# Another order for the start of a fused attention and ternary-FFN kernel: k first, q and v in one chain, the FFN weights' sums later

## The reference, cut to what matters

```python
# x: (8, 1024, 512) f32;  H = 8 heads of 64, segments of L = 128 tokens
q, k, v = xs @ Wq, xs @ Wk, xs @ Wv
# per segment, carrying a memory (mem, z) along the sequence:
sq, sk = elu(q) + 1, elu(k) + 1
att_mem = sq @ mem / (sq @ z)
mem, z  = mem + sk^T v, z + sum(sk)
att     = gate * att_mem + (1 - gate) * softmax(q k^T / 8) @ v
x = layernorm(x + att @ Wo)

def _quantize(W):                       # a threshold over the whole matrix
    gamma = mean(abs(W))
    return clip(round(W / (gamma + 1e-5)), -1, 1)
h = relu(x @ _quantize(W1)^T + b1)      # W1: (2048, 512)
x = layernorm(x + h @ _quantize(W2)^T + b2)   # W2: (512, 2048)
```

## Time and profile before

| What | Value |
|---|---|
| time, median of 3 runs | 1899.68 us |
| profiled execution, its time | 1899.23 us |
| profiled execution, its span | 1897.3 us |
| PE busy | 1851.0 us, 98% of the span |
| DVE, ACT, POOL busy | 1447.7, 1002.5, 765.9 us |
| granted PE clock, mean | 0.992 of full |

### The profile page before, as it was taken

How to read it: one execution, slowest core, us unless ns; L and a number is a source line. 1 busy time by engine, 2 the same in 40 slices (tenths; PEclk the granted TensorE clock), 3 DMA queues, 4 the chain that set the end, 5 groups by cost and what they waited for, 6 DMA issues and landing times.

```text
span 1897.3 us, 44351 instructions
## 1 busy us (share of the span) xinstructions
PE 1851.0 (98%) x16447; PEld 1307.6 (69%) x16447; DVE 1447.7 (76%) x2935; ACT 1002.5 (53%) x2422; POOL 765.9 (40%) x775
## 2 busy tenths in 40 slices
PE   5789999999999999999999999999999999999998
PEld 3566677766677766677766677766677766677765
DVE  7777777787877787777787877777777777777774
ACT  5755544545555545555545555545555545555541
POOL 1214345444345444335444344444344444344443
PEclk9899999999999999999999999999999999999999
DMA  8412433323333323333323333323333323333110
GB/s 272 124 25 47 63 58 64 65 39 60 63 59 62 62 43 60 63 58 63 67 39 60 64 59 61 68 38 60 60 63 60 69 41 56 60 59 63 35 24 23
DMA packets 556420, 117.47 MB, mean 62 GB/s; under 512 B 529824, under 2 KB 533808, under 8 KB 555696
## 3 DMA queue, kind: packets, MB, share of 16 engines
q1 hardware_dynamic: 556208, 114.64, 31.4%
HBM read 50.54 MB, written 16.80 MB: 35 GB/s over the span
## 4 chain that ended last, share of the span: by engine, by line
PE 93%; DVE 4%; ACT 2%; issue 1%; DMA 0%; POOLq 0%; SPq 0%; DVEq 0%; POOL 0%; ACTq 0%
PE bank L427 12%; PE bank L426 12%; PE bank L440 12%; PE bank L441 11%; PE bank L276 6%; PE bank L278 6%; PE bank L277 6%; PE bank L364 3%; PE bank L409 3%; PE bank L408 3%; PE bank L407 3%; PE bank L290 3%; PE bank L343 3%; PE bank L291 3%; PE bank L292 3%; PE bank L395 2%
## 5 line engine op out<-in xcount | busy, mean ns | idle before, releaser
L426 PE MATMUL bank<-yt,w1t 128*128 128x256 f16 x2048 | 453.9, 273 | 0.2 <-DVE yt L802 0.2
L427 PE MATMUL bank<-yt,w1t 128*128 128x256 f16 x2048 | 453.9, 273 | 0.0
L1145 ACT ACTIVATE prob<-bank,exp_bias,gscalars 128x128 f32<-128x128 f32 x512 | 227.6, 454 | 363.6 <-DVE exp_bias L719 358.6
L440 PE MATMUL bank<-w2t,arena 128*128 128x512 f16 x1024 | 388.4, 379 | 0.0
L441 PE MATMUL bank<-w2t,arena 128*128 128x512 f16 x1024 | 388.1, 379 | 0.0
L1189 ACT ACTIVATE arena<-bank,b_scaled,wscalars 128x256 f32<-128x256 f32 x512 | 263.1, 570 | 207.9 <-PE bank L427 155.0
L854 DVE CAST arena<-arena 128x512 f16<-128x512 f32 x256 | 153.8, 601 | 93.2 <-ACT arena L1189 92.5
L1312 POOL TENSOR_TENSOR att_mem<-att_mem,gate_in 128x512 f32<-128x512 f32 x60 | 87.1, 1452 | 330.9 <-DVE att_mem L758 319.9
L426 PEld LDWEIGHTS bank<-yt,w1t 128*128 128x128 f16 x2048 | 200.4, 98 | 23.5 <-issue 0.6
L427 PEld LDWEIGHTS bank<-yt,w1t 128*128 128x128 f16 x2048 | 200.3, 98 | 22.8
L1390 POOL TENSOR_TENSOR arena<-arena 128x512 f16<-128x512 f32 x128 | 155.2, 1213 | 86.9 <-DVE arena L854 86.9
(11 more groups left out here) (186 smaller groups left out, 4300.4 us busy)
## 6 DMA issues: line engine op xcount, KB each, us to landing
rows<-in_L_attn_x SPq DMA_DIRECT2D x32, 512.0 KB, 3.8
out_rows<-rows SPq DMA_DIRECT2D x64, 256.0 KB, 2.3
x_blocks<-in_L_attn_x SPq DMA_DIRECT2D x248, 64.0 KB, 3.0
sk<-sk_t SPq DMA_DIRECT2D x480, 32.0 KB, 2.0
att_dot<-att_mem SPq DMA_DIRECT2D x480, 32.0 KB, 2.0
y_blocks<-rows SPq DMA_DIRECT2D x480, 32.0 KB
arena<-in_L_ffn_W SPq DMA_DIRECT2D x6, 1024.0 KB, 5.4
w2t<-in_L_ffn_W SPq DMA_DIRECT2D x2, 1024.0 KB, 13.1
```

Of the source, the lines that this page charges most:

```text
L426: pe.matmul(ps[:, c], w1t[:, k, cols], yt[:, g % 2, :, k], start=k == 0, stop=False)
L427: ins = pe.matmul(ps[:, c], w1t[:, k, cols], yt[:, g % 2, :, KT + k], start=False, stop=k == KT - 1)
L440: pe.matmul(banks[own][:], h_hi[:, f, toks], w2t[:, f, :], start=f == 0, stop=False)
L1145: ins = act.activation(prob[:, t, at], ps[:, c], ACT.Exp, scale=gcol(g, G_EXP), bias=exp_bias[:, t, at:at + 1], accum_out=row_sum[:, t, h: ...
```

## The change

Only the order of the first trip changes, with two small joins; POOL and SP keep their lists word for word.

- The chains of q and v become one: PE turns both columns of maxima, the four small operations work on two cells, one product spreads both.
- k's first half is projected on PE ahead of that chain; DVE finds both maxima in a row before it; v's split comes ahead of k's second half; v is projected and split ahead of the first scores.
- o's maximum and chain come behind the first scores' maxima, and o's split on ACT comes behind the whole first softmax.
- ACT's sums, DVE's two sums and `threshold(1)` come later, among and behind the first attention's steps; `ffn_scale` comes behind `round_w(1)`.

```diff
         W_ORDER = "kqvo"
+        CHAINS = ("k", "qv", "o")
+        W_CHAIN = {n: c for c, names in enumerate(CHAINS) for n in names}
...
+            def turn_max(c):
+                if c:
+                    pe.wait_ge(sem["wscale"], c)
+                for i, n in enumerate(CHAINS[c]):
+                    pe.wait_ge(sem["wmax"], W_ORDER.index(n) + 1)
+                    ins = pe.transpose(banks[7][0:1, i * P:(i + 1) * P], w(WMAX[n]), ident32[:])
+                ins.then_inc(sem["wrow"], 1)
...
@@ PE, the loop @@
                 project_qk(g, "k", 0)
                 if g == 0:
-                    turn_max(2)
+                    turn_max(1)
+                    turn_bias()
+                    spread_max(1)
...
+                if g == 0:
+                    project_v(g, 0)
+                    project_v(g, 1)
                 scores(g, 0)
...
+                if g == 0:
+                    turn_max(2)
                 turn_p(g, 0, 0)
                 ffn_down(g - 2, 0, 1)
                 if g == 0:
-                    spread_bias_max()
+                    spread_max(2)
                 ffn_down(g - 2, 0, 2)
                 scores(g, 1)
...
-                if g == 0:
-                    sum_all(1)
                 ffn_down(g - 2, 1, 1)
                 turn_p(g, 0, 1)
+                if g == 0:
+                    sum_all(1)
+                    turn_bias_max()
                 turn_p(g, 1, 0)
+                if g == 0:
+                    spread_bias_max()
                 turn_y(g - 1, 0)
                 turn_p(g, 1, 1)
...
@@ DVE @@
             w_max("q")
-            w_chain("q")
-            w_scale("q")
+            w_max("v")
             for live in range(LIVE):
                 reset_memory(0, live)
-            w_max("v")
-            w_chain("v")
-            w_scale("v")
+            w_chain(1)
+            w_scale(1)
             scalars(0, 0)
             scalars(0, 1)
             scalars(0, 2)
+            w_split("q", 0)
+            w_split("q", 1)
             for g in range(NG + 2):
...
                 qk_split(g, "k", 0)
                 if g == 0:
-                    w_split("q", 1)
+                    w_split("v", 0)
+                    w_split("v", 1)
...
                 if g == 0:
-                    w_scale("o")
+                    v_split(g, 0)
+                    v_split(g, 1)
                 score_max(g, 0, 0)
+                if g == 0:
+                    score_max(g, 0, 1)
+                    w_max("o")
+                    w_chain(2)
                 group_max(g + 1)
                 if g == 0:
+                    w_scale(2)
                     gates()
...
                 score_max(g, 1, 1)
+                if g == 0:
+                    w_sum(2)
+                    w_sum(3)
...
                 p_split(g, 0, 1)
+                if g == 0:
+                    threshold(1)
+                    round_w(0)
+                    round_w(1)
+                    ffn_scale()
...
@@ ACT @@
             w_split("k", 1)
+            w_sum(1, 1)
             w_split("q", 0)
             w_split("q", 1)
             for g in range(NG + 2):
...
                 qk_split(g, "k", 0)
+                if g == 0:
+                    w_split("v", 0)
+                    w_split("v", 1)
                 qk_split(g, "k", 1)
...
                 qk_split(g, "q", 1)
                 if g == 0:
+                    v_split(g, 0)
+                    v_split(g, 1)
                     w_sum(1, 3)
-                    w_sum(1, 0)
-                    w_split("o", 0)
-                    w_sum(1, 2)
                 exponentials(g, 0, 0)
-                v_split(g, 0)
                 if g == 0:
-                    w_split("o", 1)
-                    w_sum(2, 0)
-                exponentials(g, 0, 1)
-                p_split(g, 0, 0)
-                v_split(g, 1)
-                exponentials(g, 1, 0)
-                exponentials(g, 1, 1)
-                p_split(g, 0, 1)
+                exponentials(g, 0, 1)
+                if g == 0:
+                    w_sum(1, 0)
+                p_split(g, 0, 0)
+                exponentials(g, 1, 0)
+                exponentials(g, 1, 1)
+                if g == 0:
+                    w_sum(1, 2)
+                p_split(g, 0, 1)
+                if g == 0:
+                    w_split("o", 0)
+                    w_split("o", 1)
+                    w_sum(2, 0)
+                p_split(g, 1, 0)
+                yt_hi(g - 1, 0)
+                p_split(g, 1, 1)
                 if g == 0:
                     w_sum(2, 1)
                     for n in range(0, 4):
                         put_w(n)
-                p_split(g, 1, 0)
...
```

More of the change, by code:

```diff
@@ L448, in turn_bias, with spread_max @@
                 pe.transpose(banks[6][:, 0:FT], b1_rows[:], ident32[0:FT, 0:FT]).then_inc(sem["bias_turn"], 1)
[L450 to L460, removed]
+            def turn_max(c):
[5 more added lines that the diff above has]
+                ins.then_inc(sem["wrow"], 1)
+            def spread_max(c):
+                first, count = WALL[CHAINS[c][0]], len(CHAINS[c])
+                if c == 0:
                     pe.wait_ge(sem["ones"], 1)
-                pe.wait_ge(sem["wchain"], 4 * at + 4)
-                pe.matmul(banks[7][:, 0:1], ones_all[0:1, :], ws[0:1, WALL[n]:WALL[n] + 1], start=True,
+                pe.wait_ge(sem["wchain"], 4 * c + 4)
+                pe.matmul(banks[7][:, 0:count], ones_all[0:1, :], ws[0:1, first:first + count], start=True,
                           stop=True).then_inc(sem["wall"], 1)
@@ L557, in _ @@
                 ffn_down(g - 2, 1, 0)
+                ffn_down(g - 2, 1, 1)
+                turn_p(g, 0, 1)
                 if g == 0:
                     sum_all(1)
-                ffn_down(g - 2, 1, 1)
-                turn_p(g, 0, 1)
+                    turn_bias_max()
                 turn_p(g, 1, 0)
+                if g == 0:
+                    spread_bias_max()
                 turn_y(g - 1, 0)
@@ L861, in w_max, with w_chain, w_scale @@
                 dve.tensor_reduce(w(WMAX[n]), raw[n], AX_XY, ALU.max, apply_absolute_value=True).then_inc(sem["wmax"], 1)
[L863 to L869, removed]
+            def w_chain(c):
+                first, count = WALL[CHAINS[c][0]], len(CHAINS[c])
+                cell = ws[0:1, first:first + count]
+                dve.wait_ge(sem["wrow"], c + 1)
+                dve.tensor_reduce(cell, banks[7][0:1, 0:count * P].rearrange("p (i n) -> p i n", n=P), AX_X,
+                                  ALU.max).then_inc(sem["wchain"], 1)
+                dve.wait_ge(sem["wchain"], 4 * c + 1)
                 dve.tensor_scalar(cell, cell, 2.0 ** -60, None, ALU.max).then_inc(sem["wchain"], 1)
-                dve.wait_ge(sem["wchain"], 4 * at + 2)
+                dve.wait_ge(sem["wchain"], 4 * c + 2)
                 dve.tensor_scalar(cell.bitcast(U32), cell.bitcast(U32), EXPONENT, None, ALU.bitwise_and).then_inc(sem["wchain"], 1)
-                dve.wait_ge(sem["wchain"], 4 * at + 3)
+                dve.wait_ge(sem["wchain"], 4 * c + 3)
                 dve.tensor_scalar(cell, cell, 2.0 ** -14, None, ALU.mult).then_inc(sem["wchain"], 1)
[L876 to L881, removed]
+            def w_scale(c):
+                inv, scale, count = INV_W[CHAINS[c][0]], SCALE_W[CHAINS[c][0]], len(CHAINS[c])
+                ps = banks[7][:, 0:count]
+                dve.wait_ge(sem["wall"], c + 1)
+                dve.tensor_copy(ws[:, inv:inv + count], ps)
+                dve.reciprocal(ws[:, scale:scale + count], ps).then_inc(sem["wscale"], 1)
             def w_split(n, j):
@@ L1007, in _ @@
                 if g == 0:
+                    w_scale(2)
                     gates()
                 normalise(g - 1, 1, 0)
-                score_max(g, 0, 1)
+                if g:
+                    score_max(g, 0, 1)
                 turn_x(g + 1, 0)
                 turn_x(g + 1, 1)
-                if g == 0:
-                    w_sum(2)
-                    ffn_scale()
                 turn_sk(g)
-                v_split(g, 0)
-                if g == 0:
-                    w_sum(3)
+                if g:
+                    v_split(g, 0)
                 invert_sums(g, 0)
-                if g == 0:
-                    threshold(1)
                 p_split(g, 0, 0)
-                v_split(g, 1)
+                if g:
+                    v_split(g, 1)
                 score_max(g, 1, 0)
```

60 lines of the change are left out of this document (16 added, 44 removed).

## The result

| | before | after |
|---|---|---|
| median (runs) | 1899.68 us | 1912.6 us (1911.59 to 1913.07, 5 runs) |
| profiled execution, its span | 1899.2, 1897.3 us | 1912.6, 1910.6 us |
| ratio to before | 1 | 1.0068, 95% interval 1.0055 to 1.0081 |

What follows compares the result with a forecast made beforehand. PE's own work was taken to bound everything behind the front, so the change is worth what it moves the front's end. 10.4 + 2.4 + 0.65 = 13.4 us on 1899.2 gave 1912.6, forecast as 1913 us; range 1908 to 1916.5.

Steps and rivals of the forecast that it cites:

- The early part: Front up to the first softmax: the new order gains, with the second half's exponentials some 8 us earlier.
- PE would stay warm through k's and v's projections: Early front: no delay of the first row maxima taken; a cold PE would make them 1 to 2 us later.
- First term: o's late split delays POOL, then the load of W2's slice 1 and ACT's first `put_w`: +10.4 us.
- the walk: Tally of ACT's and DVE's steps in the front, up to `wo_hi` at 56.0 us.
- the landing: Load of W2's slice 1, behind POOL's end of o's split: 5.4 us until it lands.
- Second term: o's split on POOL beside DVE's `round_w`: two roundings slip in between POOL's instructions and delay it, +2.4 us.
- Third term: Stretch of 32 `put_w` tiles: two `pt_hi` leave, -0.85 us; PE starts cold, +1.5 us; together +0.65 us.
- POOL was disturbed: Against the rival that POOL's o split runs undisturbed: +11.05 us, 1910.7 us; chance 0.22, shared with a shorter walk.
- PE was warm: Against the rival of PE cold through k's and v's projections: +14.9 us, 1914.6; chance 0.20, shared with more exclusion.
- The other side: Rival: the load of W2's slice 1 stays hidden, `put_w` starts at about 64 us; 1899 us, no change; chance 0.05.

Runs made afterwards that it cites:

- e2: Kernel before, with only both halves of o's split on ACT moved behind the first softmax and third `pt_hi`; ratio 1.0090.
- e4: Changed kernel, with W2's slice 1 loaded into `yt`'s room so its load needn't wait for o's split; ratio 1.0022.
- e8: Changed kernel once more, unchanged, timed on the same chip as other follow-up kernels; ratio 1.0061.
- e3: Changed kernel, with DVE's four `round_w` of W1 held until POOL ends o's split; ratio 1.0058.
- e1: Changed kernel, with ACT's two halves of o's split moved back ahead of the second half's exponentials; 1905.69 us, ratio 1.0025.
- e9: Changed kernel with own room and earlier load for W2's slice 1, earlier fourth W1 sum, last sum, o's split, threshold and rounding, later bias products; ratio 0.9997.
- e6: Changed kernel, with 40 unread matmuls on PE between the second and third `turn_w`, where it idles for the load; ratio 1.0058.
- e10: e9 with 20 unread matmuls on PE ahead of the first `turn_w`; ratio 1.0003.

## Why the prediction was right

The forecast was 1913 us, the median is 1912.6, and the profiled execution 1912.6 too. The mechanism stands: e2 makes the loss without the rest of the change, e4 removes most of it without touching the order. Its terms, step by step:

- **The early part.** Forecast: q's split at 23.0, first row maxima at 38.7, second half's exponentials at 50.1. Measured 22.38, 38.05 and 49.24: 0.6 to 0.9 early. In e8, the same kernel once more, it was 22.65, 38.84 and 50.03, so most of this is what the first loads shift from run to run. The choice that PE would stay warm through k's and v's projections held; from 20 to 37 us:

```profile
20.00:37.00 17.00, 14.87 (x124) 10.44 (x124) 12.97 (x32) 12.85 (x21) 0.00 (x0) 1.00 0.94 299
```

- **First term, +10.4.** `wo_hi` came at 55.10 (56.0 forecast), POOL's end and SP's issue were joined as said (68.91 and 68.93), and the load landed in 4.83 us, where the median of six was 5.4. Less POOL's stretching, the first `put_w` moved by 11.3 - 2.4 = 8.9 us. The term was 1.5 too high: 0.9 from the walk, 0.6 from the landing. In e8 `wo_hi` came at 55.90 and the first `put_w` at 76.72, which would leave 0.5; so only about that much is clearly an error of the term.
- **Second term, +2.4.** Measured 2.41 in POOL's four rows and 2.54 at `k_hi` (e3). The size was right, the picture behind it only half. DVE's `round_w` in after, two and two:

```profile
57.10 3.44 DVE L908 TENSOR_SCALAR w2t<-w2t,wscalars 128x2048 f32<-128x2048 f32 x2
...
63.68 3.25 DVE L908 TENSOR_SCALAR arena<-arena,wscalars 128x2048 f32<-128x2048 f32 x2
```

  Four `round_w` ran beside POOL, not two. Each pair took 3.44 and 3.25 us instead of 2.48, so DVE lost 1.7 us and POOL 2.4; both were slowed. Within each pair the first took 1.47 and 1.28 us, the second 2.05 both times (1.28 undisturbed). Had POOL kept the ports that the two share for its whole first instruction, to 59.46 us, two roundings of 1.2 would have ended at 61.9 at the earliest; they ended at 60.54. The rule of the Trainium skill ("SBUF — State Buffer", "Who interferes with whom") thus gave the right sign here and not the right rows. In e2, where DVE's pair started first, DVE lost nothing (2.47 us) and POOL's first instruction took 4.64 us instead of 2.87: there the rule's first-comer did keep the way. It did too where POOL's subtraction came first: `exp_bias` in e1 (above) ended with it, and so, a rounding's length behind, did the first `round_w` of e9:

```profile
56.60 2.12 POOL L1377 TENSOR_TENSOR wo_lo<-arena,wo_hi 128x1024 f16<-128x1024 f32 x1
56.84 2.96 DVE L912 TENSOR_SCALAR w2t<-w2t,wscalars 128x2048 f32<-128x2048 f32 x1
```

  What decides between the two cases was not tried.
- **Third term, +0.65.** Measured 28.56 - 27.20 = +1.36. The cold PE costs 1.74 (28.56 against e6's 26.82; 1.5 taken), but the two `pt_hi` that left the stretch give only 0.38 (27.20 against 26.82), not 0.85. ACT waits for PE between tiles; that it did part of that work in such waits fits, but was not tried.
- **Behind it.** 0.65 us more are lost between `k_hi` and the end, partly in PE's waits for `pt_lo` (0.6 us). No step of mine had it. In e8 it is not there: `k_hi` came 13.7 us later than in before, the end 13.3, without such waits. In the profiled execution of after the errors add up to -1.5 + 0.7 + 0.65, near zero: the agreement to half a microsecond is luck, that to 2 us isn't.
- **The rivals.** POOL was disturbed, and PE was warm; both fall. The other side, the load hidden, I had priced at 1899. e4 and e1 show that price as wrong: with the load hidden and the new order the ratio is 1.0022 and 1.0025, some 4 to 5 us above before. I had let ACT reach `put_w` by its own list at 64 us; it waits 3.9 us (e4) to 6.2 us (e1) in its two waits for the bias products and the roundings ahead of them, which I had named and held to be covered. They were, by the load.

## What to carry over

When a step is moved back, follow its buffer to the load that waits for it, and that load's place in the queue: here a 2 us split on ACT held 10 us of POOL and 5 of DMA behind it, all hidden before. Removing such a coupling is worth only the distance to the next one (here 7 to 10 of 13 us, then the bias products, then the load's place in SP's queue and its slow landing, then DVE's roundings ahead of the bias product), so read what is late next before pricing the removal. A microsecond won in the front counts as won only where it is found again at the first instruction of the steady state and in the span.

## What the runs showed that I had not expected

- Elementwise instructions on DVE and POOL slow each other by amounts that differ from row to row. In after, where POOL began, the four `round_w` lost 0.2, 0.8, 0 and 0.8 us and POOL 2.4 in all; in e2, where DVE began, DVE lost nothing and POOL 1.77 us to two; in e9 one `round_w` behind POOL's subtraction lost 1.7 us.
- 40 matmuls whose results nobody reads made the kernel after reach `k_hi` 1.6 us earlier and end 2.6 us earlier in the trace (e6), though the ratios don't tell it; 20 made no difference ahead of a wait for DVE (e10).
- The steady state, with PE busy 99.9% of it in after, lost 3.2 us to two late `pt_lo` in e3 and 2.5 in e1. Two executions of one program differ here too: 0.6 us in after, none in e8.
